# First mixture's tokens gathered by GpSimd from stored rows instead of scattered to slots, and another order in its last steps

## The reference

```
logits = relu(x @ Wr1 + br1) @ Wr2 + br2          # 8 experts
tg, ti = top_k(softmax(logits), 2); tg = softmax(tg / 2)
out = silu(x @ Ws1 + bs1) @ Ws2 + bs2             # shared expert, all tokens
for e in range(8):
    h = silu(x @ We1[e] + be1[e]) @ We2[e] + be2[e]
    out = out + sum(tg * (ti == e)) * h           # 256 -> 1024 -> 256
```

## Time and profile before

| | |
|---|---|
| median of 3 runs | 880.41 us |
| profiled execution, its time | 882.07 us |
| its span, first to last instruction | 880.1 us |
| TensorE busy | 813.7 us, 92% |
| VectorE busy | 662.6 us, 75% |
| ScalarE busy | 474.5 us, 54% |
| GpSimd busy | 249.1 us, 28% |
| mean granted TensorE clock | 0.967 |

### The profile page before, as it was taken

How to read it: one execution, slowest core, us unless ns; L and a number is a source line. 1 busy time by engine, 2 the same in 40 slices (tenths; PEclk the granted TensorE clock), 3 DMA queues, 4 the chain that set the end, 5 groups by cost and what they waited for, 6 DMA issues and landing times. The chain is left out here.

```text
span 880.1 us, 17731 instructions
## 1 busy us (share of the span) xinstructions
PE 813.7 (92%) x6055; PEld 756.6 (86%) x6055; DVE 662.6 (75%) x1356; ACT 474.5 (54%) x1004; POOL 249.1 (28%) x212
## 2 busy tenths in 40 slices
PE   8999999996999959999999999998899878999977
PEld 6887999996699959999999999995788845889877
DVE  4986999996795435888888888976887778876657
ACT  3653233232465537777777777753455542645553
POOL 8411332331005640022433333230122201532540
PEclk9998999998899979999999999997899989999999
DMA  8980000000404237577777767823000051534325
GB/s 301 300 220 1 1 0 1 0 1 4 152 1 133 103 125 286 205 223 233 239 239 237 227 214 220 293 25 102 1 0 1 0 181 33 172 103 125 105 93 178
DMA packets 55794, 111.72 MB, mean 127 GB/s; under 512 B 8306, under 2 KB 41684, under 8 KB 48948
## 3 DMA queue, kind: packets, MB, share of 16 engines
q1 hardware_dynamic: 44148, 93.29, 31.9%
q0 software_dynamic: 9408, 15.53, 7.2%
q10 hardware_dynamic: 2176, 2.10, 0.8%
HBM read 82.19 MB, written 28.70 MB: 126 GB/s over the span
## 5 line engine op out<-in xcount | busy, mean ns | idle before, releaser
L143 PE MATMUL e_ps_h<-e_xh,e_w1h 128*128 128x256 f32 (+1 forms) x496 | 141.4, 285 | 0.0
L144 PE MATMUL e_ps_h<-e_xl,e_w1h 128*128 128x256 f32 (+1 forms) x496 | 138.9, 280 | 0.0
L145 PE MATMUL e_ps_h<-e_xh,e_w1l 128*128 128x256 f32 (+1 forms) x496 | 138.5, 279 | 0.0
L2179 POOL DMA_INDIRECT accumulated<-m_yo,m_token x39 | 72.9, 1869 | 198.3 <-ACT m_yo L2320 172.4
L143 PE MATMUL e_ps_o<-e_w2h,e_hh 128*128 128x256 f32 x440 | 122.4, 278 | 0.0
L144 PE MATMUL e_ps_o<-e_w2l,e_hh 128*128 128x256 f32 x440 | 121.9, 277 | 0.0
L145 PE MATMUL e_ps_o<-e_w2h,e_hl 128*128 128x256 f32 x440 | 121.9, 277 | 0.0
L2300 ACT ACTIVATE e_hf<-e_ps_h,e_b1s 128x256 f32<-128x256 f32 (+1 forms) x248 | 98.0, 446 | 36.8 <-PE e_ps_h L145 36.8
L1064 POOL TENSOR_TENSOR at_pr<-at_pr,at_inv 128x1168 f32<-128x1168 f32 (+2 forms) x48 | 58.6, 1235 | 204.3 <-DVE at_inv L901 204.3
L144 PEld LDWEIGHTS e_ps_h<-e_xl,e_w1h 128*128 128x128 f32 x496 | 94.6, 191 | 0.0
L143 PEld LDWEIGHTS e_ps_h<-e_xh,e_w1h 128*128 128x128 f32 x496 | 94.6, 191 | 0.0
(11 more groups left out here) (425 smaller groups left out, 2277.4 us busy)
## 6 DMA issues: line engine op xcount, KB each, us to landing
e_w1s<-in_m_w SPq DMA_DIRECT2D x24, 1024.0 KB, 4.8
e_w2s<-in_m_w SPq DMA_DIRECT2D x24, 1024.0 KB, 7.1
slots_in<-zero SPq DMA_DIRECT2D x20, 258.0 KB, 9.4
e_xin<-slots_in SPq DMA_DIRECT2D x16, 258.0 KB, 4.8
last_slots_in<-zero SPq DMA_DIRECT2D x14, 258.0 KB, 8.8
d_xin<-last_slots_in SPq DMA_DIRECT2D x10, 258.0 KB, 2.8
d_results<-last_results SPq DMA_DIRECT2D x10, 256.0 KB, 5.5
as_wk<-in_a_wk SPq DMA_DIRECT2D x2, 1024.0 KB, 9.1
```

Source lines behind the costliest of these rows:

```text
L143: nc.tensor.matmul(out, lh, rh, start=start, stop=False)
L144: nc.tensor.matmul(out, lh, rl, start=False, stop=False)
L145: return nc.tensor.matmul(out, ll, rh, start=False, stop=stop)
L2179: nc.gpsimd.indirect_dma_start(out=g.acc, out_offset=bass.IndirectOffsetOnAxis(ap=token[:, n, a:a + 1], axis=0), in_=yo[:, q, a, :], in_of ...
```

## The change

- The normalised rows are stored twice, in token order, by two plain DMAs of SP (`choices_in`): once with the gates of the first choice, once with those of the second. Behind them lie 256 zero rows; only these are zeroed in the opening.
- The router's slots are inverted: VectorE compares each choice's place in its 128 slots and its unit with numberings (`places`), TensorE multiplies the two (`invert`, 32 products, ahead of step 4), VectorE makes of it for each slot the row where its choice is stored (`source`). The comparison matrices lie in weight buffers that aren't in use yet.
- GpSimd gathers a tile's rows into `xin` by one indirect DMA for each 128 slots: tiles n = 0, 1, 2 ahead of the wait for `s_acc`, and tile n + 3 at the head of the loop's turn n. SP's loads of slots, the 32 scatters and their waits go.
- At the end of the mixture TensorE does the second layer of tile 29 between the two halves of the first layer of tile 30, VectorE's `result` and ScalarE's scaling follow; the last second layer waits for each part of the hidden layer by itself.
- The scratch of the next stage is cleared one tile earlier, with the head mask and value biases made there by GpSimd; in `second_setup` ScalarE instead of VectorE writes `vbd`, ahead of its copies for A.

```diff
-SLOTS = PAIRS * ST + (SINGLES + 1) * P
+COLS = 2 * PAIRS + SINGLES + 1
...
-        rows = self.g.xs.rearrange("(a p) d -> p a d", p=P)
+        rows = self.g.xs[TOPK * TOK:].rearrange("(a p) d -> p a d", p=P)
         sp.wait_ge(self.s_zf, 3)
-        for a in range(0, rows.shape[1], 2):
-            sp.dma_start(rows[:, a:a + 2, :], self.g.zero[:]).then_inc(self.g.s_zeroed, 16)
+        sp.dma_start(rows, self.g.zero[:]).then_inc(self.g.s_zeroed, 16)
...
-        v.tensor_reduce(mask[:], g.ident[:].rearrange("p (h d) -> p h d", d=dh), AX.X, ALU.add).then_inc(s_mask, 1)
-        dve.wait_ge(s_mask, 1)
+        dve.wait_ge(early.s_blank, early.BLANKS)
...
-        dve.wait_ge(early.s_wv, 32)
-        dve.wait_ge(early.s_blank, early.BLANKS)
-        for gi in range(G):
-            dve.wait_ge(s_kv, G + gi + 1)
-            diagonal(vbd[:, :, off[gi]:off[gi] + n], ps_v(gi), bv[:, gi:gi + 1]).then_inc(s_bv, 1)
...
+        for gi in range(G):
+            act.wait_ge(s_kv, G + gi + 1)
+            for h in range(hp):
+                at = off[gi] + h * KEYS
+                last = a_.activation(vbd[:, :, at:at + KEYS], ps_v(gi).rearrange("p (b j) -> p b j", b=NB), ACT.Identity,
+                                     bias=early.bias[:, gi, h:h + 1], scale=mask[:, h:h + 1])
+            last.then_inc(s_bv, 1)
...
+    def inverse(self, w1h, w1l, w2h, w2l, w2s):
+
+        n = NT * 3 * COLS
+        self.at = [a[:, 1, :] for a in (w1h, w1l)]
+        self.of = [a[:, 1, 0:n].rearrange("p (t c u) -> p t c u", t=NT, c=3) for a in (w2h, w2l)]
+        self.iota_pos, free = w2s[:, 1, 0:P], w2s[:, 1, P:]
+        self.iota_unit, self.none = free[:, 0:COLS], free[:, COLS:2 * COLS]
+        self.iota_t, self.iota_p = free[:, 2 * COLS:2 * COLS + NT], free[:, 2 * COLS + NT:2 * COLS + NT + 1]
+
+    def places(self, dve, i):
+
+        v, pos, base, of = self.nc.vector, (self.i1, self.i2)[i], (self.p1, self.p2)[i], self.of[i]
+        wide = lambda a, n: a.rearrange("p (t x) -> p t x", t=1).to_broadcast([P, NT, n])
+        if i == 0:
+            dve.wait_ge(self.s_ids, 7)
+        v.tensor_tensor(self.at[i].rearrange("p (t x) -> p t x", t=NT), wide(self.iota_pos, P), pos[:].to_broadcast([P, NT, P]),
+                        ALU.is_equal).then_inc(self.s_at, 1)
+        v.tensor_tensor(of[:, :, 0, :], wide(self.iota_unit, COLS), base[:].to_broadcast([P, NT, COLS]), ALU.is_equal).then_inc(self.s_at, 1)
+        dve.wait_ge(self.s_at, 4 * i + 2)
+        v.tensor_scalar(of[:, :, 1, :], of[:, :, 0, :], self.iota_p, None, ALU.mult).then_inc(self.s_at, 1)
+        turn = self.iota_t.rearrange("p (t x) -> p t x", x=1).to_broadcast([P, NT, COLS])
+        v.scalar_tensor_tensor(out=of[:, :, 2, :], in0=turn, scalar=float(i * NT), in1=of[:, :, 0, :],
+                               op0=ALU.add, op1=ALU.mult).then_inc(self.s_at, 1)
+
+    def invert(self, pe, ps_i):
+
+        pe.wait_ge(self.s_at, 4 * TOPK)
+        for i in range(TOPK):
+            for t in range(NT):
+                last = self.nc.tensor.matmul(ps_i, self.at[i][:, t * P:(t + 1) * P], self.of[i][:, t].rearrange("p c u -> p (c u)"),
+                                             start=i == t == 0, stop=(i, t) == (TOPK - 1, NT - 1))
+        last.then_inc(self.s_inv, 1)
+
+    def source(self, dve, ps_i):
+
+        v, link = self.nc.vector, self.chain.link
+        flat = lambda a: a[:].rearrange("p t e -> p (t e)")
+        got, row, gap = flat(self.ex)[:, 0:3 * COLS], flat(self.pro)[:, 0:COLS], flat(self.pro2)[:, 0:COLS]
+        dve.wait_ge(self.s_inv, 1)
+        v.tensor_copy(got, ps_i).then_inc(self.s_got, 1)
+        dve.wait_ge(self.s_got, 1)
+        link(dve, v.scalar_tensor_tensor(out=row, in0=got[:, 2 * COLS:], scalar=float(P), in1=got[:, COLS:2 * COLS], op0=ALU.mult, op1=ALU.add))
+        link(dve, v.tensor_scalar(gap, got[:, 0:COLS], -1.0, 1.0, ALU.mult, ALU.add))
+        link(dve, v.tensor_tensor(gap, gap, self.none, ALU.mult))
+        link(dve, v.tensor_tensor(row, row, gap, ALU.add))
+        v.tensor_copy(self.m.rows[:], row).then_inc(self.s_rows, 1)
...
-            v.tensor_copy(m.slots[:, i, :], self.mx[:, :, 0]).then_inc(self.s_k, 1)
+            pos, base = (self.i1, self.i2)[i], (self.p1, self.p2)[i]
+            whole = pos[:].bitcast(I32)
+            link(dve, v.tensor_copy(whole, self.mx[:]))
+            link(dve, v.tensor_scalar(whole, whole, -P, None, ALU.bitwise_and))
+            link(dve, v.tensor_copy(base[:], whole))
+            link(dve, v.tensor_tensor(pos[:], self.mx[:], base[:], ALU.subtract))
...
-def scatter(nc, g, m, router, pool, s_gate):
-
-    landed = lambda i, t: 16 * (NT // 2 * i + t // 2 + 1)
-    pool.wait_ge(g.s_zeroed, 16 * (SLOTS // P // 2))
-    for i in range(TOPK):
-        pool.wait_ge(router.s_k, i + 1)
-        if i:
-            for q in range(2):
-                pool.wait_ge(m.s_sc[q], landed(i - 1, NT - 2 + q))
-            nc.gpsimd.tensor_copy(m.xn[:, :, GATE], router.gates[:, i, :]).then_inc(s_gate, 1)
-            pool.wait_ge(s_gate, i)
-        for t in range(NT):
-            if t >= 2:
-                pool.wait_ge(m.s_sc[t % 2], landed(i, t - 2))
-            nc.gpsimd.indirect_dma_start(
-                out=g.xs, out_offset=bass.IndirectOffsetOnAxis(ap=m.slots[:, i, t:t + 1], axis=0),
-                in_=m.xn[:, t, :], in_offset=None).then_inc(m.s_sc[t % 2], 16)
...
+        def gather(n):
+            q = n % 2
+            if n >= 2:
+                pool.wait_ge(s_xlo, S + n - 1)
+            for a in range(rows_of(S + n)):
+                col = 2 * n + a if n < PAIRS else PAIRS + n
+                nc.gpsimd.indirect_dma_start(
+                    out=xin[:, q, a, :], out_offset=None, in_=g.xs,
+                    in_offset=bass.IndirectOffsetOnAxis(ap=m.rows[:, col:col + 1], axis=0)).then_inc(s_xl[q], 16)
+
         router.gpsimd(pool)
-        scatter(nc, g, m, router, pool, s_gate)
+        pool.wait_ge(router.s_gated, 1)
+        pool.wait_ge(s_src, 16)
+        nc.gpsimd.tensor_copy(m.xn[:, :, GATE], router.gates[:, 1, :]).then_inc(s_gate, 1)
         for h in idle:
             pool.sem_clear(h)
+        pool.wait_ge(g.s_zeroed, 16)
+        pool.wait_ge(s_src, 32)
+        pool.wait_ge(router.s_rows, 1)
+        for n in range(3):
+            gather(n)
         pool.wait_ge(s_acc, 16 * S)
         for n in range(ROUTED):
             q = n % 2
-            if n == ROUTED - 2:
+            if n + 3 < ROUTED:
+                gather(n + 3)
+            if n == ROUTED - 3:
                 pool.wait_ge(s_w1l, unit(J - 1) + 1)
-                early.blank(nc)
+                early.blank(nc, pool)
             pool.wait_ge(s_ys, n + 1)
             if n:
                 pool.wait_ge(s_st[1 - q], stored(n - 1))
...
-                wait(sp, s_xlo, j - 1)
-                if static and j == S:
-                    for half in m.s_sc:
-                        sp.wait_ge(half, 16 * TOPK * NT // 2)
-                if rows_of(j) == 1:
-                    r0 = PAIRS * ST + (j - FIRST) * P
-                    sp.dma_start(xin[:, q, 0, :], g.xs[r0:r0 + P, :]).then_inc(s_xl[q], 16)
-                else:
-                    rows = g.xs.rearrange("(j a p) d -> j p a d", p=P, a=ROWS)
-                    rows = rows[j - S] if static else rows[bass.ds(j - S, 1)].rearrange("j p a d -> p (j a) d")
-                    sp.dma_start(xin[:, q], rows).then_inc(s_xl[q], 16)
...
+        for i in range(TOPK):
+            if i:
+                sp.wait_ge(s_gate, i)
+            else:
+                sp.wait_ge(router.s_gated, 1)
+                sp.wait_ge(router.s_ids, 1)
+            sp.dma_start(g.xs[i * TOK:(i + 1) * TOK].rearrange("(t p) d -> p t d", p=P), m.xn[:]).then_inc(s_src, 16)
         sp.wait_ge(router.s_eid, 1)
         step(S, S % 2)
+        sp.wait_ge(s_src, 16 * TOPK)
+        sp.wait_ge(s_xlo, S - 1)
...
+                        if static and j == J - 1 and mp == MP // 2:
+                            second_layer(j, q, shared)
...
+        def second_layer(j, q, shared):
+            final = isinstance(j, int) and j == J
+            common = is_shared(j - 1, shared)
+            wq = 0 if common else q
+            if not final:
+                wait(pe, s_hl, MP * j)
+            wait(pe, s_w2l, 1 if common else unit(j - 1) + 1)
+            wait(pe, s_ev, j - 2)
+            for a in range(rows_of(j - 1)):
+                o = ps_o[:, 1 - q, a, :]
+                for i in range(M1):
+                    if final and i % MG == 0:
+                        pe.wait_ge(s_hl, MP * (j - 1) + i // MG + 1)
+                    ts = slice(a * P, (a + 1) * P)
+                    last = product(nc, o, (hh[:, 1 - q, i, ts], hl[:, 1 - q, i, ts]),
+                                   (second(w2h, wq, i), second(w2l, wq, i)), i == 0, i == M1 - 1)
+            last.then_inc(s_m2, 1)
...
+            if j == 3:
+                pe.wait_ge(s_ev, 2)
+                router.invert(pe, ps_i)
```

(78 more changed lines are left out.)

27 lines of the change are left out of this document (18 added, 9 removed).

## The result

After the change the median is 1053.68 us (1046.13 to 1055.79, 4 runs) against 879.17 for the kernel before in the same series: ratio 1.196, 95% interval 1.188 to 1.204. The profiled execution has a span of 1054.0 us (before 880.1) and a mean granted clock of 0.892 (before 0.967). The forecast was 1025 us, range 955 to 1085: the right mechanism, 29 us too little.

The account below looks back on a forecast made before the run. TensorE had no idle time in routed tile steps, but a 9.3 us hole ahead of them. From the profiled 882.1, -5.0 + 119.6 + 30 gave 1027, on the median's scale 1025 us, range 955 to 1085.

Parts of the forecast that it names:

- The order on GpSimd's queue: Routed loop: each gather stands behind the previous result's scatters, so TensorE stalls every step of tiles 11 to 30; 119.6 us.
- In time: Rival for the routed steps: gathers are early enough and only the hole's removal counts; 875 us, chance 0.08.
- once only: Rival for the routed steps: the first late gather shifts the pipeline and later ones find room; 883 us, chance 0.04.
- The loop's length: Pair-tile step, from its start through two scatters, two gathers and a landing: 18.1 us against 11.55.
- The term for the landing: Second gather in a routed step, from issue to landing: 3.7 us, the middle of 2.7 and 4.8.
- The clock: Routed steps: idle holes lower the granted clock, 1.5 us each for 20 steps; 30 us, bounds 0 and 46.
- the 149.6 forecast: Tiles 11 to 30: 119.6 us of longer steps and 30 us of lost clock.
- Behind the accumulations: Rival in GpSimd's DMA queue: gathers' data wait until accumulating scatters land, 20.7 us a step; 1075 us, chance 0.13.
- The front: Ahead of the routed tiles: hole removed -11.6, VectorE's stall +2.4, TensorE's products +4.2; sum -5.0 us, bounds -11.6 to +1.
- VectorE's block: Small slot operations and first `places` ahead of tile 3's low part of x: 2.4 us TensorE stall, bounds 0 and 5.
- The end of the mixture: Tile 29's middle second layer starts tile 28's scatter 1.5 to 2 us earlier, offset elsewhere; 0, bounds -1.5 and +1.5.

Follow-up runs that it names:

- The version with the products: The changed kernel with 44 products that nobody reads ahead of TensorE's wait for each gathered tile: 1025.71 us, ratio 1.1636.
- the version without stalls: The changed kernel with gathers 0 to 4 ahead of the wait and gather n + 5 at the head of turn n: 877.12 us, ratio 0.9977.
- early masks: Gather n + 5, new end, head mask and value biases made before the shared-rows wait: 877.28 us; also with first-choice comparisons behind VectorE's step 2: 876.74 us.
- plain scatters: The changed kernel with the results' scatters overwriting instead of adding, so the output lacks the sum of the experts: 1009.89 us, ratio 1.1442.
- the gathers alone: The changed kernel with gather n + 4 at the head of turn n, and the old end of the mixture and old set-up: 886.46 us, ratio 1.0046.

## Why the prediction was right, and where it was off

*The order on GpSimd's queue* was the deciding step and held: the gather behind the scatters, the stall in every step from tile 11 on, TensorE's own transposition holding back the next scatter. One turn earlier brings the ratio from 1.196 to 1.0055, two turns to 0.9977. *In time* and *once only* are refuted by twenty waits out of twenty.

*The loop's length.* For a pair step without clock loss the prediction had 9.0 + 3.8 + 0.3 + 1.3 + 3.7 = 18.1. The version with the products shows 17.55, of which 9.0, 1.9, 1.9, 1.3 and 3.45 (start of step, scatter, scatter, gather, gather, next step). The term for the landing, bounded by 2.7 and 4.8, is off by 0.25. The other 0.3 is the first scatter's issue, 1.91 us in the earlier trace rows and 1.62 here. For single steps 13.3 was forecast and 13.2 measured.

*The clock* was somewhat under-sized: 1.5 a step was scaled down from one hole of 9.3 us. In the seven shorter pair steps the first scatter comes 10.9 into the step instead of 9.0, so 1.9. In single steps it is mostly more: the step at 706.03 takes 16.2 instead of 13.2. So the cost did not go with the length of the hole. 30 us were forecast. At least 28 are measured by filling the holes, with many left unfilled. The rows give about 12 x 1.9 = 23 for the pair steps and some 13 for the seven steps behind them, against the same steps of the version with the products: six are 0.6 to 3.6 us longer (16.85 against 16.21, 19.71 against 16.13), and one, of tile 27, is 2.2 shorter, since the version with the products lost its clock there (0.65). That makes some 36.

*Not foreseen* was the lengthening of GpSimd's issues beside VectorE's cast and subtraction: 21.9 instead of 19.5 in five of twelve steps, 12 us in all, 10 of them in the issues themselves. Of the 19.4 us by which tiles 11 to 30 exceed the 149.6 forecast, the pair steps have 10.8: 12 from the five long steps, 5 from the clock, less 7 for the shorter loop. The other 8.6 are 0.5 at tile 11 and 8.1 at tiles 24 to 30.

*Behind the accumulations* (0.13) did not happen here: 1.9 us from the end of issue to TensorE with additions or without. What failed is its price, which rested on a landing of 6.8. In the changed kernel the median accumulating scatter lands after 3.8, against 7.6 in the same stage of the kernel before, where more moves at a time (224 GB/s in a step, against 133). Its mechanism stays open: with gathers one turn earlier, where the scatters ahead took 6.0 to 8.5 us to land, no gather landed ahead of the scatter before it.

*The front* was forecast as -5.0 and is -4.7 in the changed kernel, -6.1 in the version without stalls (in the two with gathers one turn earlier -6.1 and -5.8). In the version without stalls the products and the wait behind them took 4.06 (4.2 forecast), and VectorE's block stalled TensorE for 1.5 (2.4).

*The end of the mixture*, forecast as 0 (-1.5 to +1.5), took +5.3 in the changed kernel, +0.3 with gathers two turns earlier, and with early masks +0.3 and -1.1 in the two versions that have them. The middle second layer does free the result of tile 28 earlier, but GpSimd is busy with clearing and masks until 758.1:

```profile
749.72 1.57 POOL L2242 DMA_INDIRECT accumulated<-m_yo,m_token  x1 [13.99 <-ACT m_yo L2401]
...
753.28 1.67 POOL L2587 MEMSET early_mask<- 128x4 f32 x1
...
755.02 2.27 POOL L2589 TENSOR_SCALAR_AFFINE_SELECT early_mask<-early_mask 128x4 f32<-128x4 f32 x1
...
758.41 1.59 POOL L2242 DMA_INDIRECT accumulated<-m_yo,m_token  x1 [0.28 <-issue]
...
771.72 1.44 SPq L2532 DMA_DIRECT2D X<-accumulated  x3
```

Of the 5.3 us, 4.6 are the clock again: the scatter of tile 27 starts 749.72 - 737.56 = 12.2 behind tile 30's transposition, in a stretch with a granted clock of 0.53 and no idle time of TensorE, where it was 7.6 in the earlier trace rows; with gathers two turns earlier and the same new end it is 7.6 again. The prediction had no term for the masks on GpSimd; two of their operations, on 128x4, took 3.9 us together.

## What to carry to other kernels

When a load moves onto a queue that also carries the results out, write down for each turn what stands ahead of it and from which step that comes; a prefetch three tiles ahead in the program was less than one step ahead in time, and one line's shift by two turns is worth 177 us. Place a prefetch where its buffer becomes free, not at the loop's head behind work that waits for something late. A stall that returns in every step costs more than its length, since the clock is lowered again each time (0.85 over a pair step here).

## What the hardware did that was not expected

- GpSimd's indirect DMAs have no fixed issue time: mostly 0.95 to 1.02 us (gather or plain scatter) and 1.55 to 1.64 (accumulating); beside VectorE's 1.22 us cast or 2.29 us subtraction of 128x2048 up to 2.84 and 3.56. It goes the other way too: the cast took 3.08 beside two memsets. The Trainium skill (GPSIMD Engine Reference, Specifications) says that GpSimd shares its memory interface with VectorE, which matters for VectorE instructions with two inputs in SBUF or in a faster mode that uses both ports. The rows agree as far as they go: the subtraction reads two tiles, and the cast takes about half the time of a subtraction of the same size, so it runs in a faster mode; whether that mode uses both ports no row shows. With plain scatters the gathers came earlier, and in the pair steps none took the 2.75 us that it takes beside the subtraction. But no run moved VectorE's work alone, so the cause is argued and not shown.
- A step that loses clock can follow a short stall: with gathers one turn earlier, 1.15 us of idle time ahead of 547.28 was followed by a step of 13.24 us instead of 8.3, at 0.61. The two earlier ones of 1.24 and 1.46 us were followed by full-speed steps (11.58 and 11.61), and with the gathers alone a stall of 1.07 us at the same tile by one of 8.62 at 1.00. What makes the difference was not tried, so the stall is not shown to be the cause.
- Behind accumulating scatters that took 6.0 to 8.5 us to land, a gather issued next landed with them: 18 of 18 came 0.28 to 0.34 us behind the scatter, 2.9 to 5.2 us after the end of their own issue (1.8 to 1.9 in the changed kernel, where the scatters land early).
